# A decoder block with sixteen routed experts: expert weights loaded in four chained parts, and eight buffers of weighted rows in place of four

## What is computed

```python
logits = x.astype(jnp.float32) @ gate_w.T
scores = jax.nn.sigmoid(logits)
_, topk_idx = lax.top_k(scores + expert_bias[None, :], TOP_K)        # 4 of 16
topk_w = jnp.take_along_axis(scores, topk_idx, axis=-1)
topk_w = topk_w / jnp.sum(topk_w, axis=-1, keepdims=True)
...
def _swiglu_ffn(x, wg, wu, wd):
    return jax.nn.silu(x @ wg.T) * (x @ wu.T) @ wd.T
def step(acc, ws):
    wg, wu, wd, cw = ws
    return (acc + cw[:, None] * _swiglu_ffn(x, wg, wu, wd), None)
routed, _ = lax.scan(step, jnp.zeros_like(x), (w_gate, w_up, w_down, combine.T))
shared = _swiglu_ffn(x, sw_gate, sw_up, sw_down)
return (routed + shared).reshape(orig_shape)
```

## Time and profile before

| | |
|---|---|
| device time, median of 3 runs | 1470.19 us (1468.96 to 1476.5) |
| the profiled execution, its own time | 1475.8 us |
| its span | 1474.1 us |
| TensorE busy in the span | 1308.5 us (89%) |
| VectorE, ScalarE, GpSimd busy | 837.3, 710.4, 381.9 us |
| mean granted clock of TensorE | 0.951 |
| moved by DMA | 235.59 MB |

### The profile page before, as it was taken

How to read it: one execution, slowest core, us unless ns; L and a number is a source line. 1 busy time by engine, 2 the same in 40 slices (tenths; PEclk the granted TensorE clock), 3 DMA queues, 4 the chain that set the end, 5 groups by cost and what they waited for, 6 DMA issues and landing times. The chain is left out here.

```text
span 1474.1 us, 22215 instructions
## 1 busy us (share of the span) xinstructions
PE 1308.5 (89%) x7473; PEld 1039.5 (71%) x7473; DVE 837.3 (57%) x1764; ACT 710.4 (48%) x1589; POOL 381.9 (26%) x491
## 2 busy tenths in 40 slices
PE   5899999999999759999999997996999999899960
PEld 5666776767766448888787885784888878688840
DVE  6677677677676375675666656683333333233316
ACT  4788578578667434443454443322333333233323
POOL 0234223133223110100101001102554453455420
PEclk9999999999999779999999999998999999999985
DMA  4211221212110055777667575317889999885557
GB/s 185 115 51 44 72 80 51 72 44 82 41 44 1 0 186 187 239 243 243 222 227 259 167 254 182 120 61 309 237 200 289 249 241 313 263 214 107 105 96 296
DMA packets 96907, 235.59 MB, mean 160 GB/s; under 512 B 10584, under 2 KB 47452, under 8 KB 93856
## 3 DMA queue, kind: packets, MB, share of 16 engines
q1 hardware_dynamic: 78960, 188.96, 36.5%
q0 software_dynamic: 17840, 45.22, 14.7%
HBM read 146.20 MB, written 87.95 MB: 159 GB/s over the span
## 5 line engine op out<-in xcount | busy, mean ns | idle before, releaser
L2001 PE MATMUL e_both_ps<-e_w,e_x_t 128*128 x948 | 242.5, 404 | 9.8 <-DMA e_w<-w_split 9.8
L2001 PEld LDWEIGHTS e_both_ps<-e_w,e_x_t 128*128 128x128 f32 x948 | 173.7, 190 | 46.5 <-issue 10.2
L514 PE MATMUL proj_ps<-wqkv,x_sp 128*128 128x384 f32 x768 | 173.4, 356 | 10.5 <-DVE wqkv L382 10.5
L1868 POOL DMA_INDIRECT acc_rows<-e_y,token_row x79 | 125.3, 1586 | 177.0 <-ACT e_y L1912 84.2
L1181 PE MATMUL c_score_ps<-ct,x_t 128*128 128x402 f32 x768 | 163.8, 368 | 0.0
L1204 PE MATMUL c_out_ps<-cr,weigh_t 128*128 128x512 f32 (+1 forms) x624 | 149.9, 397 | 1.4 <-DVE weigh_t L1022 1.4
L1181 PEld LDWEIGHTS c_score_ps<-ct,x_t 128*128 128x128 f32 x768 | 145.8, 200 | 5.7 <-issue 4.5
L265 POOL TENSOR_SCALAR_AFFINE_SELECT p_t<-p_t 128x128 f32<-128x128 f32 x256 | 87.3, 353 | 220.3 <-ACT p_t L359 216.4
L1937 DVE TENSOR_TENSOR e_x_t<-e_turn_ps,e_x_t 128x512 fp32r<-128x512 f32 x79 | 54.5, 691 | 153.5 <-ACT e_x_t L1899 153.5
L514 PEld LDWEIGHTS proj_ps<-wqkv,x_sp 128*128 128x128 f32 x768 | 132.2, 195 | 11.9 <-issue 10.5
L1204 PEld LDWEIGHTS c_out_ps<-cr,weigh_t 128*128 128x128 f32 (+1 forms) x624 | 115.8, 188 | 28.7 <-issue 1.7
(11 more groups left out here) (233 smaller groups left out, 2253.1 us busy)
## 6 DMA issues: line engine op xcount, KB each, us to landing
e_w<-w_split SPq DMA_DIRECT2D x15, 3072.0 KB, 12.8
w_split<-c_piece SPq DMA_DIRECT2D x96, 384.0 KB, 3.5
c_piece<-w_experts SPq DMA_DIRECT2D x96, 192.0 KB, 3.7
raw<-ctxT SPq DMA_DIRECT2D x16, 800.5 KB, 4.4
w_split<-rows SPq DMA_DIRECT2D x24, 512.0 KB, 3.4
raw<-ctx_rows SPq DMA_DIRECT2D x16, 768.0 KB, 5.0
acc_rows<-rows SPq DMA_DIRECT2D x8, 1024.0 KB, 9.1
rows<-w_experts SPq DMA_DIRECT2D x24, 256.0 KB, 2.7
```

The lines of the kernel that those rows point to most:

```text
L514: mm = nc.tensor.matmul(proj_ps[:, tt, 0:GW], x_sp[:, xs, c, tt * P:(tt + 1) * P], wqkv[:, ws, c, hg * GW:(hg + 1) * GW], start=(c == 0 an ...
L1868: nc.gpsimd.indirect_dma_start(acc[m % 2], bass.IndirectOffsetOnAxis(ap=token_row[:, 1, m:m + 1], axis=0), y[:, m % YB, :], None, compute_ ...
L2001: mm = nc.tensor.matmul(both_ps[:, m % 2, :], x_t[:, m % 2, xs, c * P:(c + 1) * P], weights(slot, ws, c * GU, (c + 1) * GU), start=(c == 0 ...
```

## The change

`load(n)` issues its 3 MiB as four DMAs (`PARTS` = 4), each of a quarter of the columns: 128 rows of 6,144 bytes. SP waits for each to land ahead of issuing the next one; the count that it waits for goes up by 16 for each part. After the last part `loaded` is counted up as before. Load 0, which GpSimd issues, stays whole. The number of buffers `y` goes from 4 to 8, by which `weigh_y(m)` waits for scatter m-8.

```diff
         XG = 6
-        YB = 4
+        YB = 8
+        PARTS = 4
         GU = 2 * I
...
                 if n >= RING:
                     sp.wait_ge(down_done, sp.value_load(free_at[0:1, n - RING:n - RING + 1], min_val=1,
                                                         max_val=TILES + 1))
-                sp.dma_start(slot_of(n), split_weights(expert)).then_inc(w_in[n % RING], 16)
-                sp.wait_ge(w_in[n % RING], 16 * (n // RING + (n % RING > 0)))
+                earlier = n // RING - (n % RING == 0)
+                for k in range(PARTS):
+                    cols = slice(k * 2 * WE // PARTS, (k + 1) * 2 * WE // PARTS)
+                    sp.dma_start(slot_of(n)[:, cols], split_weights(expert)[:, cols]).then_inc(w_in[n % RING], 16)
+                    sp.wait_ge(w_in[n % RING], 16 * (earlier * PARTS + k + 1))
                 sp.sem_inc(loaded, 1)
```

## The result

The changed kernel took **1534.01 us** (median of 4 runs, 1530.16 to 1538.42), the kernel before, beside it on the same chip, 1472.78 (1468.96 to 1476.5): a ratio of **1.0408, with a 95% interval of 1.0372 to 1.0445**. It is slower, as forecast, but by 61 us and not by 12, and so far outside the range of 1461 to 1497.

What follows compares the result with a forecast made beforehand. The prediction took TensorE to bound the routed stage, with 11.9 us of stands behind scatters. It summed -11.9 - 4 + 19.4 + 3 + 2 = +8.5 us, and forecast 1482 us, range 1461 to 1497.

Steps and rivals of the forecast that it cites:

- The stands behind scatters, -11.9: Routed stage, tiles 1 to 76: eight buffers and smaller packets remove all five TensorE stands behind slow scatters, 11.9 us.
- The start, -4: Tile 0's wait for expert 0's weights: load 1 in parts shares the engines less, saving 4 us, between 0 and 5.
- Three further starts at 2.45: Each chained load on SP: three further part starts at 2.45 us each, 7.35 us more per load.
- The other traffic in a load: Loads 5 to 11: scatters let through lengthen three of the seven loads by 2.2 us each, 6.5 more.
- its upper bound: Each load's parts: one 0.18 us packet let in per part packet, 23.4 us a load, 31 us late; chance 0.05.
- the forecast's rate for loads 12 to 14: Loads 12 to 14 follow at 22.3 us each, 66.8 in all against 63.1 of tiles: 3 us more (0 to 9).
- the 19.4: Tile 44, first of expert 11: load 11 comes 19.4 us late, after 34.6 us of spare time is used up.
- tens of us to spare: nothing: Loads 2 to 4 and 15: tens of us of spare time, so their lengthening costs nothing.
- The restarts, +2: TensorE after a long stand: restarts at a lower granted clock; two restarts cost 2 us.
- The rival in which scatters stay slow: Scatters no faster, the 11.9 us stay but mostly overlap waits for weights: 1484 to 1490 us; counted within slower, no separate chance.
- The rival in which the parts hide and only the savings are left: Part starts overlap scatter traffic and load 11 comes in time: faster, 1454 to 1462 us; chance 0.2.
- the chosen story: Late chained loads replace scatters as the routed stage's bound: slower; chance 0.5, plus 0.05 for the upper bound.

## Why the prediction was right in sign and wrong in size

**The stands behind scatters, -11.9: right.** They are gone, and the scatters land in 4.6 to 9.5 us, 5.6 at the median, near the 5 to 8 of the forecast. But of the two reasons given one falls. The eight buffers do nothing alone, nor beside parts, chained (1533.51 us with four buffers) or not (1457.36). The other, packets of scatters and load that alternate one for one, does not hold in a chained load: 1220 passed beside 576, and 302 beside 144 in the one part. That scatters and gathers get more of the engines than beside a whole load fits the runs that have no such stands, but was not tested by itself. (The five stands lie ahead of tiles 26, 34, 47, 49 and 51; the forecast has the last three one tile late, which changes no sum.)

**The start, -4: right in size**, 5.2 measured, but not by the step that was argued. The first part of load 1 did not lie ahead of the stretch shared with expert 0: issued at 1004.88, it landed only just before 1019.31, when the second was issued, and tile 0 had started at 1018.82. So expert 0's load met one part of load 1, the first. Tile 0 started at 1018.8 and not near 1021; 1.4 us of that is the earlier stage. Load 1 landed some 10 us later, not 6. TensorE did not wait for it, as said; GpSimd's wait for the shared result's stores grew from 18.5 to 27.7 us.

**Three further starts at 2.45: right**, as far as the runs show: 2.5 was measured where no scatters ran, whatever the smaller packets cost included. The rule of the Trainium skill (page "DMA: Bandwidth & Descriptors", sections "Bandwidth" and "Anatomy of one DMA": 1 MiB or more to a DMA, about 2.0 us fixed to each, fitted there to DMAs that GpSimd issues) points the same way and nearly at the same price; this case's number, for DMAs that SP issues, is 2.5. By the rule alone the loss would have been smaller still than the forecast's.

**The other traffic in a load: this term failed.** The forecast's load was 11.4 us, 7.35 for the starts and 2.2 for traffic, some 21; its upper bound let one small packet past each of a part's eight, 1.4 us a part. (With the 4.3 us of a part that is 5.7, not the 5.85 it went on with; the bound stays near.) Measured beside a running TensorE a load is 11.4 + 7.4 + 8.0 = 26.8 us: the scatters put in 26.8 - 18.8 = 8.0, 2.0 a part, beyond that bound. The bound has 8 x 16 x 4 = 512 packets of the others in a load; 1220 passed. The slip is in the premise: the traffic in a load of the kernel before (0.55 MB in 11.5 us, 0.048 MB per us, in the load shown) was read as what the traffic needs, while it was what a full load queue left it. What it needs stood in the earlier trace rows, 58.1% of the engines and 0.107 MB per us, and beside the chained load it gets that; the forecast used the row only to lean towards its upper half. But that demand by itself doesn't make a load long, since beside four queued parts the others get 0.097 and the load takes 14.4 us. It is dear together with the chain: per load, no packet of it is on its way for 7.3 us, where it was 1.8 with all parts queued and 5.7 with the chain but no scatters.

**What came of it, by the forecast's own steps.** At 22.3 us from load to load, the forecast's rate for loads 12 to 14, the ten loads 2 to 11 would have ended 10 x 22.3 = 223 us behind 1035.2, at 1258, and tile 44, due without stands at 1025.5 + 43 x 4.855 = 1234.3, would have been 24 late, near the 19.4. At 25.9 they ended at 1294.0, 60 us late: the 36 us more are 10 x 3.6. The same step made loads 2 to 4 safe in the forecast ("tens of us to spare: nothing"). Tile 19 was due at 1025.5 + 18 x 4.855 = 1112.9; at 22.3 us load 4 would have come at 1102, 11 us early, less than the tens claimed, and at 27 to 29 us a load it came 4.9 late. From there on the chain had no slack, where the forecast began to count at load 5 with 34.6 us of it. Load 14 was 15.4 late, not 3.

**The restarts, +2: too small**, 9.4, for there were five stands behind tile 0 and not two, and a restart cost 1.7 to 2.7 us and not 1 (that of tile 43 is in the 16.3 us ahead of tile 44). In the windows of the changed kernel the ten us from 1223 (us; busy us of PE, PEld, DVE, ACT, POOL; granted clock, DMA share, GB/s) have the clock at 0.68, a mix of 1.2 and 2.4 GHz as in the earlier trace rows:

```profile
1223.00:1233.00 10.00, 9.10 (x31) 7.33 (x32) 1.27 (x4) 1.83 (x4) 0.53 (x1) 0.68 0.49 144
```

The order of the late tiles (43 or 44, then 57), the waits for slots that vanish, and the chain of loads as the new bound came as forecast; the stands at tiles 19 and 37 did not, nor did the loads of 20 to 22 us. The rival in which scatters stay slow did not come: they land in 9.5 us at most, and the 11.9 us are gone. The rival in which the parts hide and only the savings are left (1454 to 1462) is not this kernel, but it is the one without the chain: 1458.59 and 1457.36.

**Against the chosen story.** That the waits between parts make a load long beside scatters is shown: by loads of 15.5, 17.4 and 24.7 us with four, two and one part in flight, and by 18.8 with the chain but no scatters. That the empty queue is the larger part of it (5.5 of 9.2 us) is counted in the traces. The shares of the engines (44.5% and 55.5% for the others) show less than they seem to, since in bytes they are 0.097 and 0.107 MB per us. Why packets of a chained load move more slowly even while they move, and how the engines choose between the two queues, stays open.

## What to carry to other kernels

A wait between two DMAs of one stream empties its queue, and beside other traffic that costs more than the fixed start: a load here had 5.7 us without a packet on its way when no scatters ran, 7.3 when they did, and 1.8 when all parts were queued. So price a chained transfer with the other traffic at what it asks for, read where no transfer runs (0.107 MB per us here), and not at what it got beside a full queue (0.048 in the load shown). To let small transfers past a large one, cut the large one into several DMAs of smaller packets and keep them all queued; then the others got 0.097 MB per us, and the load still took only 15.5 us.

## What the runs showed of the hardware

Cutting a load's one DMA into four, all of them queued, and its packets from 24.6 to 6.1 KB raised the others' share beside it from 31% to 42% over loads 2 to 15 (from 20.6% to 44.5% in the two loads shown), and the load's duration only from 12.9 to 15.5 us. And the same 768 KB took 5.8 to 6.2 us as 32 rows of 24.6 KB but 4.6 to 4.8 as 128 rows of 6.1 KB while TensorE stood: few large rows in a DMA are the slower form.
